# The low parts of the polar stage made by GpSimd instead of VectorE, and two loads put ahead of the last batch's stores

## What is computed

```python
q_mag = jax.nn.softplus(q)
k_mag = jax.nn.softplus(k)
qp = freqs[None, None, :, :]
kp = freqs_with_bias[None, :, :, :]
q_embed = jnp.stack([q_mag * jnp.cos(qp), q_mag * jnp.sin(qp)], axis=-1).reshape(B_, H, S_, 2 * D)
k_embed = jnp.stack([k_mag * jnp.cos(kp), k_mag * jnp.sin(kp)], axis=-1).reshape(B_, H, S_, 2 * D)
scores = jnp.einsum('bhsd,bhtd->bhst', q_embed, k_embed) / D ** 0.5
attn = jax.nn.softmax(scores, axis=-1)
```

## Time and profile before

| what | value |
|---|---|
| median of 3 runs | 1791.13 us (1790.16 to 1791.51) |
| profiled execution | 1783.87 us, its span 1782.1 us |
| mean granted TensorE clock | 0.941 |
| busy over the span | PE 90%, DVE 69%, ACT 73%, POOL 29% |

### The profile page before, as it was taken

The page is one execution under the profiler, slowest core; times in us unless marked ns, Lnnn a source line. Parts: engine busy times, 40 slices in busy tenths (PEclk is TensorE's granted clock), DMA queues, the critical chain, the costliest instruction groups (busy, mean ns, idle before and its releaser), DMA issues. The chain is left out here.

```text
span 1782.1 us, 38929 instructions
## 1 busy us (share of the span) xinstructions
PE 1610.2 (90%) x14430; PEld 759.7 (43%) x14430; DVE 1222.9 (69%) x2499; ACT 1295.8 (73%) x2201; POOL 515.6 (29%) x916
## 2 busy tenths in 40 slices
PE   7899996875999999989799999788878999999998
PEld 4676674751233333337533333345431333333356
DVE  4777777799999999948601100146669999999743
ACT  5655653795688888876689999657764888888863
POOL 4422423642322223224300000023332222322352
PEclk9899997885899999999989999899986999999999
DMA  4000000045332232300131111001243222222101
GB/s 127 1 1 1 1 1 1 1 138 177 92 77 74 76 80 76 81 2 19 49 95 57 56 58 58 1 18 56 84 118 98 59 63 62 62 59 58 30 7 42
DMA packets 119489, 98.74 MB, mean 55 GB/s; under 512 B 30347, under 2 KB 109509, under 8 KB 119301
## 3 DMA queue, kind: packets, MB, share of 16 engines
q1 hardware_dynamic: 110052, 95.15, 18.8%
q0 software_dynamic: 8192, 0.77, 0.9%
q10 hardware_dynamic: 1056, 0.33, 0.1%
HBM read 63.82 MB, written 31.59 MB: 54 GB/s over the span
## 5 line engine op out<-in xcount | busy, mean ns | idle before, releaser
L1597 ACT ACTIVATE m_probs<-m_psum 128x512 f32<-128x512 f32 (+1 forms) x768 | 513.9, 757 | 87.1 <-PE m_psum L1523 81.3
L1597 ACT ACTIVATE e_probs<-e_psum 128x512 f32<-128x512 f32 x512 | 277.3, 597 | 72.4 <-PE e_psum L1523 66.5
L1641 DVE TENSOR_REDUCE a_minus_max<-m_psum 128x1 f32<-128x512 f32 x512 | 316.3, 681 | 11.3 <-PE m_psum L1532 10.8
L1641 DVE TENSOR_REDUCE a_minus_max<-e_psum 128x1 f32<-128x512 f32 x512 | 315.7, 681 | 10.7 <-PE e_psum L1532 10.4
L1523 PE MATMUL m_psum<-m_q_stack,m_k_stack 114*32 114x512 bf16 (+1 forms) x4096 | 294.5, 385 | 7.5 <-DMA m_k_stack<-n_parts 4.3
L1543 PE MATMUL m_psum<-m_probs,m_v_ones 128*32 128x512 f32 x2048 | 270.0, 600 | 2.5 <-ACT m_probs L1597 1.7
L1523 PEld LDWEIGHTS m_psum<-m_q_stack,m_k_stack 114*32 114x32 bf16 (+1 forms) x4096 | 100.7, 96 | 213.9 <-issue 115.1
L1523 PE MATMUL e_psum<-e_q_stack,e_k_stack 126*32 126x512 bf16 x2048 | 157.8, 384 | 2.1 <-ACT e_probs L1597 2.1
L1543 PE MATMUL e_psum<-e_probs,e_v_ones 128*32 128x512 f32 x1024 | 132.5, 593 | 1.0 <-ACT e_probs L1597 0.8
L1587 DVE COPY m_ctxT<-m_psum 128x512 f32<-128x512 f32 x16 | 11.1, 692 | 172.6 <-PE m_psum L1543 172.6
L1532 PE MATMUL m_psum<-m_k_stack,m_q_stack 48*128 48x512 bf16 x512 | 113.8, 399 | 17.0 <-DVE a_minus_max L1641 17.0
(11 more groups left out here) (423 smaller groups left out, 2763.2 us busy)
## 6 DMA issues: line engine op xcount, KB each, us to landing
polar_q<-m_late SPq DMA_DIRECT2D x24, 256.0 KB, 3.0
polar_k<-m_late SPq DMA_DIRECT2D x24, 256.0 KB, 3.4
m_q_stack<-polar_q SPq DMA_DIRECT2D x64, 96.0 KB, 2.3
m_k_stack<-polar_k SPq DMA_DIRECT2D x64, 96.0 KB, 2.4
m_q_stack<-dist_parts SPq DMA_DIRECT2D x192, 32.0 KB
m_k_stack<-dist_parts SPq DMA_DIRECT2D x192, 32.0 KB
gate_parts<-e_late SPq DMA_DIRECT2D x24, 256.0 KB, 3.0
e_q_stack<-gate_parts SPq DMA_DIRECT2D x64, 72.0 KB
```

Of the source, the lines that this page charges most:

```text
L1597: act.activation(self.buf.probs[(NT * m + c) % self.buf.PROBS][:, self.WIDE * part:self.WIDE * (part + 1), :], self.ps_s[i % self.PAIRS], ...
L1641: dve.tensor_reduce(self.minus_max[n % 2][:, k:k + 1], ps[:, :], AX.X, ALU.max, negate=True).then_inc(self.bank_free, 1)
```

## The change

GpSimd makes all the low parts. In GpSimd's step s, after what stood there, it makes both low parts of batch s-9 for batches 0 to 6; those of batch 7 come after the fills and `set_up`, ahead of the attention. VectorE's two calls are guarded by a constant that is 0, so it makes none. `low` waits besides for the low part of the batch before. SyncE issues the loads of groups 2 and 3 ahead of the stores of batch 7, not behind them. In the last group the loads are written in another way; SyncE's order there is the same row for row.

```diff
-    def low(self, dve, b):
-        dve.wait_ge(self.mid_ready, b + 1)
-        dve.tensor_tensor(self.part(b, 2), self.left(b), self.part(b, 1), ALU.subtract).then_inc(self.lo_ready, 1)
+    def low(self, eng, b):
+        eng.wait_ge(self.mid_ready, b + 1)
+        wait_ge(eng, self.lo_ready, b)
+        eng.tensor_tensor(self.part(b, 2), self.left(b), self.part(b, 1), ALU.subtract).then_inc(self.lo_ready, 1)
...
+    POOL_LOWS = 0
...
         for b in batch(s, 10):
-            prep.split[0].low(dve, b)
+            if b < self.POOL_LOWS:
+                prep.split[0].low(dve, b)
...
         for b in batch(s, 10):
-            prep.split[1].low(dve, b)
+            if b < self.POOL_LOWS:
+                prep.split[1].low(dve, b)
...
+    def low(self, pool, b):
+        for split in self.prep.split:
+            split.low(pool, b)
...
-                for b in range(NB):
+                for b in range(NB - 1):
                     polar.store(sp, b)
...
                 first.load(sp, 2)
                 first.load(sp, 3)
+                polar.store(sp, NB - 1)
...
                     polar.gpsimd(pool, s)
+                    for b in batch(s, 9):
+                        if b < NB - 1:
+                            polar.low(pool, b)
...
                 buf.set_up(pool)
+                polar.low(pool, NB - 1)
...
                 for s in range(gated.STEPS):
+                    if s == NB + 3:
+                        attention.load(sp, 2)
+                        attention.load(sp, 3)
                     gated.store(sp, s)
...
-                    for u in FILLS.get(s, ()):
-                        attention.load(sp, u)
+                    if s in (NB - 1, NB):
+                        attention.load(sp, s - NB + 1)
```

## The result

| | before | changed |
|---|---|---|
| median of 12 runs | 1790.03 us (1783.25 to 1792.2) | 1794.0 us (1791.64 to 1798.68) |
| ratio, 95% interval | | 1.0036, 1.0022 to 1.0049 |
| profiled execution; span | 1783.87; 1782.1 us | 1794.19; 1792.4 us |
| mean granted TensorE clock | 0.941 | 0.940 |

The change makes the kernel slower, by 0.36% or, as the ratio has it, 6.4 us (between 3.9 and 8.8, so clear of zero). The two medians lie 4.0 us apart, the means of the 12 runs 6.1: the direction is sure, the size only to some 2 us.

A forecast was written before the change was run, and what follows sets the result against it. It took the polar stage and first attention's start as deciding, VectorE and ScalarE near their limit. Step 2 late by X + 0.7 - 1.1 (+1.3, about +4.6 or +11.6); +10 likeliest on median 1791.13, so 1801 us; range 1792 to 1807.

The forecast's parts named there:

- The new wait: Polar steps 10 to 13: queries' `rest(b)` waits for GpSimd's `low(b-2)` behind scale and bias, some 4 us a step.
- My 2.2 us between `aggregate` and `rest`: VectorE, step 11: time from the end of `aggregate` to `rest`, 3.36 us less 1.14 for the second L448.
- the faster rival: Polar stage: GpSimd's first low part is done before `rest`, VectorE's relief comes through; step 2 4.5 us earlier, 1786.6; chance 0.10.
- The port: Polar stage: large two-input instructions of GpSimd and VectorE take turns; a lost turn costs `rest` one low part, 2.4 us.
- The length of a low part: GpSimd's 1024-element two-input instruction, taken as 2.4 us from rows of 256 and 512 elements; 4.8 us a batch.
- The sum of four rounds: Polar steps 10 to 13: lateness of the queries' `rest`, 7.0 us from waits, plus 4 x 2.4 from the port.
- The upper case: Polar stage: the second low part takes the port before `rest` in each of four rounds; 16.6 us late at `rest` of batch 5.
- X: End of polar stage: lateness at `embed_k(7)`, after two L448 (2.3 us) are gone; 1.7, about 5, or 12 us.
- The moved loads: SyncE, end of polar stage: group 2's loads ahead of batch 7's stores end TensorE's 1.07 us wait; -1.1 us.
- The forecast of 1801: Whole kernel: +10 us taken as likeliest gives 1801 us; the forecast itself, +6 to +13 (1797 to 1804), had 0.50.
- the mild rival: Polar stage: `rest` wins the port each time or conflicts hardly count; +1.3 to +4.6 us, 1792.4 to 1795.7; chance 0.30.
- the row for small instructions: Polar stage: L315 within GpSimd's L245 kept its 0.19 us, so nothing was counted; the skill's rule would add some 4 us.

The follow-up runs named there:

- e10_queries_only: Changed kernel with only the queries' low parts on GpSimd, the keys' on VectorE; ratio 1.0028 to the kernel before.
- e7_keys_only: Changed kernel with only the keys' low parts on GpSimd, the queries' on VectorE; ratio 0.9978 to the kernel before.
- e2_order_kept: Changed kernel with SyncE's old order, batch 7's stores ahead of the loads of groups 2 and 3; ratio 1.0048 to the kernel before.
- e5_last_late: Changed kernel with batch 7's low parts behind the split and sending of group 0's max rows on GpSimd; ratio 1.0021 to the kernel before.
- e1_order_alone: Kernel before with only SyncE's new order, loads of groups 2 and 3 ahead of batch 7's stores; ratio 0.9996 to the kernel before.
- e9_keys_first_late: Changed kernel, only keys' low parts on GpSimd, ahead of the scale, the last behind group 0's max rows; ratio 0.9975 to the kernel before.
- e11_queries_first_late: Changed kernel, only queries' low parts on GpSimd, ahead of the scale, the last behind group 0's max rows; ratio 1.0006 to the kernel before.
- e6_first_and_late: Changed kernel, low parts of batches 0 to 6 ahead of the scale, batch 7's behind group 0's max rows; ratio 0.9977 to the kernel before.
- e8_port_alone: Kernel before plus 14 unread subtractions on GpSimd where the change puts low parts of batches 0 to 6; ratio 1.0044 to the kernel before.
- e3_low_first: Changed kernel with low parts of batches 0 to 6 ahead of the norms' scale in GpSimd's step; ratio 1.0000 to the kernel before.

## Why the prediction was right, and where its sizes were off

**The new wait: right.** It was named as `rest(b)` of the queries for `low(b-2)` behind scale and bias, some 4 us; it is 3.86 in steps 12 and 13, and e10_queries_only has it at 3.55, e7_keys_only, without the queries' low parts on GpSimd, not at all. In steps 10 and 11 I had put it on `rest` too, and there it fell on the router's L315 and L317, through the port. The lateness is the same, since `rest` comes when GpSimd's second low part is done in either case. In e2_order_kept and e5_last_late step 11 does show the expected form, `rest` begun 2.0 us earlier and 3.06 us long, and it ends within 0.1 us of where it ends in the changed kernel, counted from the reference row. But another engine pays besides: ScalarE waits 2.10 us for L317. My 2.2 us between `aggregate` and `rest` took it that removing L448 would bring `rest` forward; L307 kept its place, held by TensorE. The sum does not need this number, the faster rival does.

**The port: right in the case I chose.** `rest` loses it both times that it is let go by the semaphore, 0.1 us after GpSimd's next has begun: 3.07 us against 1.21. I took a turn to add 2.4 us, and it adds 1.9: a low part lasts 2.12, and the second is already under way when `rest` comes.

**The length of a low part: a little high.** I took 2.4 us, from rows of 256 and 512 elements. The group of all sixteen, by shape:

```profile
L449 POOL TENSOR_TENSOR m_late<-m_late 128x1024 bf16<-128x1024 f32 x16 | 37.3, 2351 | 8.0 <-ACT m_late L444 7.5 <-POOL m_v_ones L1389 0.2
```

The mean of 2.35 is drawn up by those that meet VectorE (one pair lasts 5.20, above); one by itself takes 2.12 (4.23 for a pair), 12% less than taken. The slope between two sizes was drawn from instructions with f32 outputs, and this one writes bf16; whether that is the difference was not tried.

**The sum of four rounds: the term that was mis-sized.** The upper case had 16.6 us at the end of `rest(5)`; the trace has 10.6 + 1.85 = 12.5, in steps of 3.8, 3.3, 3.4 and 2.0 where I had 4.4, 4.2, 4.5 and 3.5. Each round has two low parts, so their length makes 0.56 a round, 2.2 of the 4.1. Some 1.6 is in VectorE's part of the rounds, from `rest` to the end of `aggregate`, which I had left as in the earlier trace rows less one L448: 7.6 us instead of 8.0 (376.11 to 383.74, and the same in the next round), and 6.3 instead of 7.1 in the last. Before, VectorE stood there for TensorE's L365 (0.18 us in step 10, 1.37 in step 12); in the changed kernel, late as it is, it no longer does. The remaining 0.3 is the overlap of `rest` with the end of the second low part.

**From there on each step held.** From the end of `rest(5)` to `embed_k(7)` I gave back 4.6 us (16.6 to 12), and 4.5 was given back (12.5 to 8.0). `turn_rows` was to be X + 0.7, and is X + 0.9; here two errors cancel, for the low parts of batch 6 end 5.0 us behind the end of `embed_k(7)` and not 4.4 (they meet VectorE), and those of batch 7 take 4.2 and not 4.8. I also counted six L448 removed behind `embed_k(7)`; they are four, the other two being in X already, which changes no term. The moved loads were to give 1.1, and by e1_order_alone they do; in the changed kernel's trace only 0.35 of it is seen, since TensorE waits 0.71 us more for what the profile calls its own issue. None of the nine other kernels with the new order has that gap: from `turn_rows` to step 2 it is 5.5 to 5.6 us in all of them, and 6.3 here. What stood there in this one execution was not settled. With 4.1 less in the rounds, 0.2 more at `turn_rows` and 0.75 more behind it, 11.6 becomes the 8.5 measured.

**The forecast of 1801.** It was +10 on 1791.13. The trace says +8.5 and the times +6.4; and the median before, now over 12 runs, is 1790.03, 1.1 lower. The range, from 1792 to 1807, held, but 1794.0 lies under the narrower 1797 to 1804, and by its number alone it falls to the mild rival (1792.4 to 1795.7). The traces decide against that rival: `rest` does not win the port, and step 2 is 8.5 us late and not 1.3 to 4.6. What the traces of the stage do not give is why the times move by less than step 2 does in the slowest kernels (12.2 and 12.1 us late, 8.6 and 7.9 us in the times). One execution has been traced of each kernel, and the part from L176 to the end lasted between 998.9 and 1006.5 us in the thirteen traces, in no order that goes with the change (1000.7 before, 1000.3 in the change, 1004.8 in e1_order_alone, which differs from before in nothing there). The granted TensorE clock goes with it: between 400 and 500 us behind L176 it is 0.97 or 0.98 in the eight traces whose last part takes 998.9 to 1003.4 us, and 0.91 or 0.92 in the five of 1004.3 to 1006.5. The same holds from run to run. In one series of 29 runs the kernel before took 1783.1 us at a mean clock of 0.943, and 1793.4 at 0.934, and e9_keys_first_late had 0.942 in the mean of its runs where e11_queries_first_late had 0.938. So one and the same kernel gives 1783 and 1793 us, and a difference of a few microseconds in the times is not all the stage's. Whether the lower clock makes the part longer or both have a third cause, and whether the kernels bring it about, was not tried and stays open.

**The rival that was nearest to being true.** "Faster: GpSimd keeps up", 4.5 us earlier at step 2, had a chance of 0.10, and for the change as made that was fair: what it needed, the first low part done in time for `rest`, was out of reach (in step 10 it ends 6.1 us after `aggregate`, and `rest` could have come at 4.4, behind the router: 371.54 plus the 0.84 from L307 to `rest` before). But the 6.7 us in which GpSimd waits for `aggregate` stood in the earlier trace rows, and e6_first_and_late, which uses them, comes 4.3 us earlier. The worth of the move lay in its place, not in its engine.

**The rule of the Trainium skill** (SBUF — State Buffer, "SBUF: two separate sides") says that the one that starts first keeps the shared pair for the whole of its instruction. For what is on the port with a 1024-element instruction the trace agrees at any size: `rest` with 1024 elements and L315 with 32 both end with GpSimd's L449 or its end plus their own length. Against GpSimd's four-element L245 the rows do not show it: L315 runs its 0.19 us from 372.91, where L245 lasts from 372.03 to 373.06 (e8_port_alone), as in the earlier trace rows; both rows meet only L245's last 0.2 us, so this says little, and the prediction gave the row more weight than it bears. I had gone "by the row for small instructions", as if the size of the one that is held mattered. It does not: the router's are as small as they come and are held in full.

## What to carry to other kernels

Before work is moved to an engine that has time, look in its timeline for when in the step it has that time, and who waits for it last: the idle stretch here lay ahead of a wait, and the work was put behind it. A buffer with two copies turns the mover's lateness into a wait of the engine that was to be relieved; pick first the half whose reader comes late (the keys here). And look for instructions that have grown, not for waits alone: of the 12.5 us lost up to `rest(5)`, 7.1 came in two steps in which two instructions of 0.19 us lasted 2 each.

## What the runs showed of the hardware that was not expected

- VectorE's smallest two-input instructions are held up by GpSimd's large ones in full: L315 and L317, 32 elements, 0.19 us alone, last 1.92 and 2.17 beside L449 in step 10, 1.90 and 2.16 in step 11. It goes both ways: GpSimd's L247, four elements, lasts 1.26 us beside VectorE's L635, and 0.20 without.
- An instruction of VectorE with one input in PSUM is not held up: L343 keeps its 0.67 us at 366.99 in e3_low_first, wholly within an L449 (366.33 to 368.46), and L377 its 0.69 at 400.93, within another (400.02 to 402.16). In no trace is such an instruction (L343, L377, L608) in the polar stage longer within a low part than elsewhere.
- When GpSimd has two such instructions in a row and the first lets VectorE go by a semaphore, GpSimd's second has the port first: `rest` lasts 3.07 and 3.06 us in the two cases of the changed kernel, and 3.06 or 3.07 in the six of e2_order_kept and e5_last_late.
- GpSimd subtracts 128x1024 of f32 and bf16 into bf16 in 2.12 us, where VectorE takes 1.22; one f32 table from itself takes it 1.96.
